# A spectral tokenizer on one core: the row inverse inside the main loop, row transform and mixing in banks of their own, mixing at 32 columns

## The chip, the cores and the metric

The kernel runs on one core of a Trainium2 chip. The metric is device time in microseconds (us) of one execution; lower is better. The kernel before has a median of 5176.1 us over 3 runs (5170.6 to 5191.34).

## What is computed

Sixty-four images of 64 x 64 pixels with 3 channels go through a tokenizer of four Fourier layers and then through two transformer-like blocks (attention, gated experts). Only the tokenizer is touched. Its reference, cut:

```python
h = layer_norm(x @ fc0_w + fc0_b)                # 32 channels
for i in range(4):
    X = rfft2(h)                                 # over the 64 x 64 pixels
    Y[:12, :12]  = einsum('bixy,ioxy->boxy', X[:12, :12],  w1[i])
    Y[-12:, :12] = einsum('bixy,ioxy->boxy', X[-12:, :12], w2[i])
    h = irfft2(Y) + einsum('bchw,oc->bohw', h, conv_w[i]) + conv_b[i]
    h = layer_norm(h)                            # over channels
    if i < 3: h = gelu(h)
h = gelu(h @ fc1_w + fc1_b); h = gelu(h @ fc2_w + fc2_b); h = h @ fc3_w + fc3_b
```

Everything is fp32. The kernel computes the Fourier transforms as products with small tables, and only for the 24 x 12 modes that are kept.

## The kernel before, in words

The images are worked on in 4 groups (loop over `g`) of 16, each group in two units (`u` = 0, 1) of 8 images. A unit's activations stay in `h`. A stage of a unit consists of these steps, which TensorE (PE) carries out in the order in which they are written, each filling PSUM banks that VectorE (DVE) and ScalarE (ACT) empty:

- **row inverse** (`pe_inverse`, L398 to L412, product L408): 8 banks of 16 products with the table `inv_r`, alternately in `aux[0]` and `aux[1]`; `drain_inverse` (L578) copies the even ones to `zq` on DVE and the odd ones on ACT. At its end PE waits until all are copied (L411).
- **main loop** (`pe_main`, L414): 16 chunks of 512 columns in six banks (`main[0..3]`, `aux[0..1]`): column inverse from `zq` (L431, two row halves at a time) plus pointwise convolution of `h` (L434). ACT squares a chunk (L696), DVE sums (L678), POOL or DVE (`dve_newton`) makes the inverse root, DVE scales into `xn` (L669). Five chunks later (`LAG`) PE transposes it back (L442) into `tp[0]`, ACT applies gain and GELU and writes `h` (L708), PE transposes `h` (L450) into `tp[1]`, and ACT copies that to `pix` (L714). The last iterations of the loop, c = 16 to 21, have no chunk products left, only the two transposes ("the tail" below).
- **forward** (`pe_forward`, L454): the column transform A (L481, 8 banks of 8 products in `aux`, copied to `t_w`), the row transform B (L496, 4 banks of 12 products in `aux`, each copied to `xs` by four copies of 32 partitions), and the mixing of channels (L510, 6 banks of 24 products in `aux`, weights `mixw` of 64 columns, two output halves in turn). Each product streams 64 columns of `xs`, of which the upper 32 are overwritten by the next product. Before mixing, PE waits until all of B has been copied (L500). `drain_forward` (L586) copies on DVE (j = 0) and ACT (j = 1); at its end DVE makes a negated copy (L627), on which SyncE's queue (SP) waits (`sp_spectrum`, L759): it writes the mixed spectrum to DRAM in 8 transfers and loads it back transposed into `yd`, from which the next row inverse of the same unit reads.

Stage 0 (embedding) has no inverse: its chunks are L424, and it transposes `h` afterwards (L467) instead of in the loop. Then a hardware loop runs over three layers `l`, each for both units (inverse, main, forward); the fourth layer (`last`) has inverse and main alone, and an MLP (L544, L554, L563) ends the group. So a group has 8 forwards, 8 inverses and 10 main loops. Counters (`aux_full`, `aux_free`, `main_free`, ...) order the engines; `base_of` gives their values. An fp32 product is two records each of weight load and of product in the profile.

Of the kernel before, what the change touches and what calls it, by code (L numbers as in the profile page):

```python
# [15 lines left out]
LAYERS, M1, M2 = 4, 12, 12  # L16
# [12 lines left out]
AX_EMBED, AX_ROWS, AX_A, AX_B, AX_MIX, AX_C = 1, 4, 4, 2, 3, 4  # L29
# [3 lines left out]
AX_LAYER = UNITS * (AX_C + AX_FWD)  # L33
AX_LAST = UNITS * AX_C
AX_GROUP = AX_STAGE0 + (LAYERS - 1) * AX_LAYER + AX_LAST + UNITS * AX_MLP

# [71 lines left out]
def tokenizer(nc, t, tok, named):  # L108
# [9 lines left out]
    with ctx:  # L118
# [17 lines left out]
        XC = KX * KQ * 2 * MODE  # L136
        xs = sb("xs", [128, XC + MODE])

# [14 lines left out]
        start = sb("start", [1, 24])  # L153
# [53 lines left out]
        with nc.Block() as block:  # L207
# [116 lines left out]
            def _(pe):  # L324
# [4 lines left out]
                for l in range(LAYERS):  # L329
# [7 lines left out]
                                  "tp_full", "tp_free"))  # L337
        aux_full = [sem(f"aux_full{i}") for i in range(2)]
# [15 lines left out]
        xv = xs[:, 0:XC].rearrange("p (x n b k a) -> p x n b k a", x=KX, n=2 * KQ, b=NB, k=4)  # L354
# [7 lines left out]
        def base_of(g, s, u, l=None):  # L362
# [8 lines left out]
            return chunks, g * AX_GROUP + (START + done + u * (AX_C if s == LAYERS else AX_LAYER // 2))  # L371
# [26 lines left out]
        def pe_inverse(pe, g, s, u, l):  # L398

            _, n = base_of(g, s, u, l)  # L400
            stage = l if l is not None else s - 1
            pe.wait_ge(yd_in[u], (g * LAYERS + stage + 1) * 16)
            for k in range(2 * AX_C):
                j, a, e = k % 2, k // 2, k % 2
                pe_aux(pe, j, n + k // 2)
                for i in range(8):
                    for half in range(2):
                        mm = pe.matmul(aux[j][64 * half:64 * half + 48, 64 * i:64 * i + 64], ydv[:, u, 8 * e + i, :, :, a].rearrange("p s n -> p (s n)"),  # L408
                                       inv_r[:, 64 * half:64 * half + 64], start=True, stop=True, skip_group_check=True)
                mm.then_inc(aux_full[j], 1)  # L410
            for j in range(2):  # L411
                pe.wait_ge(aux_free[j], n + AX_C)  # L412

        def pe_main(pe, g, s, u, l):  # L414

            m, _ = base_of(g, s, u, l)
            layer = l if l is not None else s - 1
            turns = l is not None
            for c in range(NCH + LAG + (1 if turns else 0)):
                if c < NCH:  # L420
                    bank = wide[c % 6]
                    if s == 0:
# [22 lines left out]
                if turns and c > LAG:  # L445
# [6 lines left out]
                    mm.then_inc(turn_full, 1)  # L452

        def pe_forward(pe, g, s, u, l):  # L454
            m, n = base_of(g, s, u, l)
            if s == 0:
# [17 lines left out]
            else:  # L474
                n = n + AX_C
# [1179 lines left out]
```

## Time and profile before

| | before |
|---|---|
| median of 3 runs | 5176.1 us |
| the profiled execution | 5172.52 us |
| its span | 5170.7 us |
| PE busy | 4003.1 us (77%) |
| PE weight loads busy | 3068.6 us (59%) |
| DVE busy | 2241.4 us (43%) |
| ACT busy | 2084.0 us (40%) |
| POOL busy | 1057.9 us (20%) |
| granted PE clock, mean | 0.904 |

The page of the profile gives shares of the whole span, in which the tokenizer's stages and the blocks behind it are mixed. What a change in one stage is worth is read from that stage: its rows on the time axis, the gaps before them (in brackets, with who ended them), and the clock in those microseconds.

### The profile page before, as it was taken

The page shows a single profiled execution, that of the slowest core. Times are in us where ns is not written, and L with a number is a line of the kernel's source. Part 1 is how long each engine was busy: PE and PEld are TensorE (multiplying, and loading weights), DVE is VectorE, ACT ScalarE, POOL GpSimd, SP SyncE. Part 2 cuts the span into 40 slices and gives each one's busy share as a digit, 9 for nine tenths or more (in the row PEclk, how much of TensorE's full clock was granted, in tenths as well). Part 3 has the DMA queues.
Part 4 walks back from the last instruction along what each step waited for, and adds up shares of the span by engine and source line. Part 5 has one row for each costly group of instructions (what it writes and reads, how often), then busy time and mean ns, then how long its engine had stood idle before and what let it go on. Part 6 is the DMA issues. An engine that isn't in the chain of part 4 may idle for free. (4 is left out here: it accounts for less than half of the span.)

```text
span 5170.7 us, 101350 instructions
## 1 busy us (share of the span) xinstructions
PE 4003.1 (77%) x39344; PEld 3068.6 (59%) x39344; DVE 2241.4 (43%) x4535; ACT 2084.0 (40%) x3050; POOL 1057.9 (20%) x700
## 2 busy tenths in 40 slices
PE   0278888896788888967888889778888896867258
PEld 0167777742677777526777775267777751763146
DVE  6543433431434334315334334153343331687666
ACT  1243443355434433555334335553343355221112
POOL 0122321321213212203122123031231230000120
PEclk9989999998899999888999999889999988878679
DMA  9402102200021012000120120001201201000000
GB/s 214 135 20 75 57 20 66 66 1 15 19 73 59 20 57 75 1 15 20 59 73 20 57 65 11 14 21 56 75 20 57 74 1 30 2 1 0 0 1 9
DMA packets 168686, 213.28 MB, mean 41 GB/s; under 512 B 156402, under 2 KB 158679, under 8 KB 159874
## 3 DMA queue, kind: packets, MB, share of 16 engines
q1 hardware_dynamic: 166514, 182.84, 12.1%
q10 hardware_dynamic: 1680, 23.60, 1.8%
q8 instruction: 343, 5.62, 0.5%
q14 instruction: 149, 1.22, 0.1%
HBM read 147.28 MB, written 59.12 MB: 40 GB/s over the span
## 5 line engine op out<-in xcount | busy, mean ns | idle before, releaser
L725 POOL TENSOR_TENSOR rstd<-var,mhalf 128x16 f32<-128x16 f32 x320 | 931.2, 2910 | 44.1 <-POOL var L722 4.4
L722 POOL TENSOR_TENSOR var<-ssum,eps 128x16 f32<-128x16 f32 x320 | 69.4, 217 | 3179.7 <-DVE ssum L678 3179.7
L678 DVE TENSOR_REDUCE ssum<-sq 128x16 f32<-128x512 f32 x640 | 437.6, 684 | 502.5 <-ACT sq L696 493.1
L708 ACT ACTIVATE h<-tp,gb 128x512 f32<-128x512 f32 x640 | 550.5, 866 | 144.4 <-PE tp L442 141.6
L442 PE MATMUL tp<-ident,xn 128*128 128x128 f32 x2560 | 434.3, 299 | 182.6 <-DVE xn L669 113.0
L442 PEld LDWEIGHTS tp<-ident,xn 128*128 128x128 f32 x2560 | 326.7, 154 | 294.0 <-DVE xn L669 207.4
L481 PE MATMUL aux<-fwd_w,pix 128*128 128x96 f32 x4096 | 469.7, 277 | 23.2 <-ACT pix L714 16.2
L434 PEld LDWEIGHTS main<-convw,h 128*128 128x128 f32 x3072 | 391.9, 202 | 154.8 <-issue 154.8
L481 PEld LDWEIGHTS aux<-fwd_w,pix 128*128 128x128 f32 x4096 | 464.7, 194 | 30.5 <-ACT pix L714 21.9
L696 ACT ACTIVATE sq<-main 128x512 f32<-128x512 f32 x480 | 288.2, 600 | 474.7 <-PE main L434 425.0
L569 DVE COPY t_w<-aux 128x384 f32<-128x384 f32 (+1 forms) x224 | 105.7, 472 | 792.5 <-PE aux L481 491.2
L434 PE MATMUL main<-convw,h 128*128 (+1 forms) x3072 | 440.5, 293 | 0.0
L408 PE MATMUL aux<-inv_r,yd 96*48 96x64 f32 x8192 | 387.7, 262 | 40.6 <-issue 40.6
L408 PEld LDWEIGHTS aux<-inv_r,yd 96*48 96x48 f32 x8192 | 382.6, 189 | 44.7 <-issue 44.7
L510 PE MATMUL aux<-xs,mixw 128*64 128x64 f32 x9216 | 322.9, 240 | 86.1 <-ACT xs L569 86.1
L569 ACT COPY t_w<-aux 128x384 f32<-128x384 f32 (+1 forms) x224 | 91.9, 410 | 735.5 <-PE aux L481 428.1
L510 PEld LDWEIGHTS aux<-xs,mixw 128*64 128x64 f32 x9216 | 319.4, 153 | 90.4 <-issue 90.4
L431 PE MATMUL main<-zq,inv_w 48*128 48x512 f32 x768 | 282.8, 661 | 64.6 <-DVE xn L669 38.2
L669 DVE TENSOR_TENSOR xn<-main,rstd 128x512 f32<-128x512 f32 x480 | 324.2, 682 | 17.5 <-PE tp L442 14.0
L450 PE MATMUL tp<-ident,h 128*128 128x128 f32 x1536 | 235.7, 277 | 23.5 <-ACT pix L714 23.5
L569 DVE COPY xs<-aux 32x288 f32<-32x288 f32 x256 | 164.4, 642 | 169.4 <-PE aux L496 166.8
L714 ACT COPY pix<-tp 128x512 f32<-128x512 f32 x384 | 221.3, 576 | 17.9 <-PE tp L450 17.9
(223 smaller groups left out, 5547.3 us busy)
## 6 DMA issues: line engine op xcount, KB each, us to landing
mixw<-mix_scratch SPq DMA_DIRECT2D x16, 4608.0 KB, 18.7
y_scratch<-t_w SPq DMA_DIRECT2D x256, 144.0 KB
yd<-y_scratch SPq DMA_DIRECT2D x32, 1152.0 KB, 7.3
mix_scratch<-mixw SPq DMA_DIRECT2D x64, 288.0 KB, 4.7
mixw<-mix_scratch ACTq DMA_DIRECT2D x1, 4608.0 KB, 13.7
h<-in_L_tok_w1r ACTq DMA_DIRECT2D x6, 576.0 KB, 10.4
h<-in_L_tok_w1i ACTq DMA_DIRECT2D x6, 576.0 KB, 10.3
h<-in_L_tok_w2r ACTq DMA_DIRECT2D x6, 576.0 KB, 18.3
```

The source lines that it names most:

```text
L408: mm = pe.matmul(aux[j][64 * half:64 * half + 48, 64 * i:64 * i + 64], ydv[:, u, 8 * e + i, :, :, a].rearrange("p s n -> p (s n)"), inv_r[ ...
L431: pe.matmul(wide[(c + half) % 6][:, :], inv_w[rows, :], zq[rows, 256 * c:256 * c + 512], start=True, stop=False)
L434: mm = pe.matmul(bank[:, 128 * i:128 * i + 128], h[:, (u * S + 4 * c + i) * 128:(u * S + 4 * c + i) * 128 + 128], convw[:, layer, :] if l ...
L442: mm = pe.transpose(tp[0 if turns else d % 2][:, 128 * i:128 * i + 128], xn[:, d % 2, 128 * i:128 * i + 128], ident[:, :])
L481: mm = pe.matmul(aux[j][:, 48 * i:48 * i + 96], pv[:, c0 + i, 2 * ap:2 * ap + 2, :].rearrange("p a r -> p (a r)"), fwd_w[:, :], start=True ...
L510: mm = pe.matmul(aux[j][64 * half:64 * half + 64, MODE * x:MODE * x + 2 * MODE], mv[:, half, part, x0 + x, y, :], xs[:, at:at + 2 * MODE], ...
L569: return eng.tensor_copy(out, in_) if j == 0 else eng.copy(out, in_)
L669: dve.tensor_tensor(xn[:, d % 2, :].rearrange("p (n c) -> p n c", c=CH), wide[d % 6][:, :].rearrange("p (n c) -> p n c", c=CH), rstd[:, d ...
L678: dve.tensor_reduce(ssum[:, c % 4, :], sq[:, c % 2, :].rearrange("p (n c) -> p n c", c=CH), AX.X, ALU.add).then_inc(red_done, 1)
L696: act.activation(sq[:, c % 2, :], wide[c % 6][:, :], ACT.Square, scale=CH ** -0.5 / (CUBIC if c % 4 >= 2 else 1)).then_inc(sq_full, 1)
L708: act.activation(out, in_, fn, bias=gb[:, 1, stage:stage + 1] if l is None else gb[:, 1, bass.ds(stage, 1)], scale=gb[:, 0, stage:stage + ...
L725: pool.tensor_tensor(rstd[:, c % 4, :], var[:, c % 4, :], mhalf[:, :], ALU.pow).then_inc(rstd_done, 2)
```

## The change

Three edits. (1) The row inverse is no longer a step of its own ahead of a unit's main loop. It is issued inside the main loop of the unit before it, from iteration 15 on: one bank each in c = 15 to 18, two each in c = 19 and 20 (`inv_banks`), behind the transposes of that iteration, with counters of its own (`inv_full`, `inv_free`). DVE empties its banks between the last three scalings, ACT behind its copy to `pix`. Unit 1's inverse lies in unit 0's loop, unit 0's next one in unit 1's loop. Stage 0's second unit takes the first inverse. (2) A uses `main[0..1]`. B is grouped by thirds of the column modes: six banks of its own (`row_bank`), four products each, each bank copied by four copies of 32 partitions as before (24 copies of 32 x 192 in all instead of 16 of 32 x 288). `xs` is laid out by those thirds, and the mixing of a third waits only for its two banks; mixing too has six banks of its own (`mix_bank`), and the next main loop waits for them bit by bit (`AUX_AT`). (3) A mixing product streams 32 columns instead of 64. The numbers of products are the same throughout.

```diff
-AX_EMBED, AX_ROWS, AX_A, AX_B, AX_MIX, AX_C = 1, 4, 4, 2, 3, 4
+AX_EMBED, AX_ROWS, AX_A, AX_B, AX_MIX, AX_C = 1, 4, 4, 3, 3, 4
...
-        XC = KX * KQ * 2 * MODE
-        xs = sb("xs", [128, XC + MODE])
+        XC = 2 * KX * MODE
+        xs = sb("xs", [128, KQ * (XC + MODE)])
...
+        def inv_of(g, u, stage):
+
+            return g * (LAYERS * UNITS * AX_C) + stage * (UNITS * AX_C) + (START + u * AX_C)
+
+
+        def inv_banks(c):
+            return {NCH - 1: (0,), NCH: (1,), NCH + 1: (2,), NCH + 2: (3,), NCH + 3: (4, 5), NCH + 4: (6, 7)}.get(c, ())
...
+        def mix_bank(k):
+            return (main[0], main[1], main[2], main[3], tp[0], tp[1])[k]
+
+        def row_bank(y, b):
+            return ((main[2], main[3]), tp, aux)[y][b]
...
+        def pe_inverse(pe, g, u, stage, m, k):
+
+            j, a, e = k % 2, k // 2, k % 2
+            n = inv_of(g, u, stage)
+            if k == 0:
+                pe.wait_ge(yd_in[u], g * (LAYERS * 16) + stage * 16 + 16)
+                pe.wait_ge(main_free, m + 12)
+            pe.wait_ge(inv_free[j], n + k // 2)
+            for i in range(8):
+                for half in range(2):
+                    mm = pe.matmul(aux[j][64 * half:64 * half + 48, 64 * i:64 * i + 64], ydv[:, u, 8 * e + i, :, :, a].rearrange("p s n -> p (s n)"),
+                                   inv_r[:, 64 * half:64 * half + 64], start=True, stop=True, skip_group_check=True)
+            mm.then_inc(inv_full[j], 1)
...
+        AUX_AT = {0: 2, 2: 1, 4: 0}
...
+            if s > 0:
+                for j in range(2):
+                    pe.wait_ge(inv_free[j], inv_of(g, u, layer) + AX_C)
             for c in range(NCH + LAG + (1 if turns else 0)):
                 if c < NCH:
                     bank = wide[c % 6]
+                    if s > 0 and c in AUX_AT:
+                        for j in range(2):
+                            pe.wait_ge(aux_free[j], n - AUX_AT[c])
...
+                if nxt is not None:
+                    for k in inv_banks(c):
+                        pe_inverse(pe, g, *nxt, m, k)
+
+        def pe_forward(pe, g, s, u, l, nxt):
             m, n = base_of(g, s, u, l)
+            if nxt is not None:
+                for j in range(2):
+                    pe.wait_ge(inv_free[j], inv_of(g, *nxt) + AX_C)
...
-                    mm = pe.matmul(aux[j][:, 48 * i:48 * i + 96],
+                    mm = pe.matmul(main[j][:, 48 * i:48 * i + 96],
                                    pv[:, c0 + i, 2 * ap:2 * ap + 2, :].rearrange("p a r -> p (a r)"),
                                    fwd_w[:, :], start=True, stop=True, skip_group_check=True)
                 mm.then_inc(aux_full[j], 1)
+            done = n
             n = n + AX_A
-            for j in range(2):
-                pe.wait_ge(aux_free[j], n)
+            for y in range(KQ):
+                for b in range(NB):
+                    rows = row_bank(y, b)[:, 0:192].rearrange("p (s a n) -> p s a n", s=2, a=2)
+                    for ap in range(2):
+                        if y == 0 and b == 0:
+                            for j in range(2):
+                                pe.wait_ge(aux_free[j], done + AX_A // 2 * (ap + 1))
+                        for part, table in enumerate((fwd_re, fwd_im)):
+                            mm = pe.matmul(rows[:, :, ap, :], tv[:, ap, b, part, 4 * y:4 * y + 4].rearrange("p k c -> p (k c)"),
+                                           table[:, :], start=(part == 0), stop=(part == 1), skip_group_check=True)
+                    mm.then_inc(aux_full[b], 1)
 
             if u == 0:
                 pe.wait_ge(mixw_in, (g * LAYERS + (0 if s == 0 else (l + 1)) + 1) * 16)
-            for k in range(2 * AX_B):
-                j, ap, b = k % 2, k // 2, k % 2
-                pe_aux(pe, j, n + k // 2)
-                for y in range(KQ):
-                    for part, table in enumerate((fwd_re, fwd_im)):
-                        mm = pe.matmul(aux[j][:, 96 * y:96 * y + 96], tv[:, ap, b, part, 4 * y:4 * y + 4].rearrange("p k c -> p (k c)"),
-                                       table[:, :], start=(part == 0), stop=(part == 1), skip_group_check=True)
-                mm.then_inc(aux_full[j], 1)
-            n = n + AX_B
-            for j in range(2):
-                pe.wait_ge(aux_free[j], n)
             for k in range(2 * AX_MIX):
                 j, y, x0 = k % 2, k // 2, M1 // 2 * (k % 2)
-                pe_aux(pe, j, n + k // 2)
+                bank = mix_bank(k)
+                if j == 0:
+                    for b in range(NB):
+                        pe.wait_ge(aux_free[b], n + y + 1)
                 for x in range(M1 // 2):
                     for part in range(2):
                         for half in range(2):
-                            at = (((half * M1 + x0 + x) * KQ + y) * 2 + part) * MODE
+                            at = y * (XC + MODE) + (part * KX + half * M1 + x0 + x) * MODE
                             flat = k == 0 and x == 0 and half == 0
-                            mm = pe.matmul(aux[j][64 * half:64 * half + 64, MODE * x:MODE * x + 2 * MODE],
-                                           mv[:, half, part, x0 + x, y, :], xs[:, at:at + 2 * MODE],
+                            mm = pe.matmul(bank[64 * half:64 * half + 64, MODE * x:MODE * x + MODE],
+                                           mv[:, half, part, x0 + x, y, :], xs[:, at:at + MODE],
                                            start=(part == 0), stop=(part == 1 and not flat), skip_group_check=True)
                     if k == 0 and x == 0:
-                        mm = pe.matmul(aux[j][0:64, 0:MODE], biasw[:, :],
+                        mm = pe.matmul(bank[0:64, 0:MODE], biasw[:, :],
                                        dc[:, 0, :] if s == 0 else dc[:, bass.ds(l + 1, 1), :].rearrange("p l n -> p (l n)"), start=False, stop=True, skip_group_check=True)
                 mm.then_inc(aux_full[j], 1)
...
+        def drain_inverse(eng, j, g, u, stage, k):
+            n = inv_of(g, u, stage)
+            a, e = k // 2, k % 2
+            eng.wait_ge(inv_full[j], n + (k // 2 + 1))
+            copy(eng, j, zv[0:112, :, a, :, e, :],
+                 aux[j][0:112, :].rearrange("p (i d r) -> p r d i", i=8, d=2)).then_inc(inv_free[j], 1)
...
-            for k in range(j, 2 * AX_B, 2):
-                ap, b = k // 2, k % 2
-                eng.wait_ge(aux_full[j], n + (k // 2 + 1))
+            for y in range(KQ):
+                eng.wait_ge(aux_full[j], n + y + 1)
                 for ky in range(4):
                     rows = slice(32 * ky, 32 * ky + 32)
-                    out = xv[rows, :, :, b, ky, 2 * ap:2 * ap + 2].rearrange("p x n a -> p n a x")
-                    ins = copy(eng, j, out, aux[j][rows, 0:288].rearrange("p (n a x) -> p n a x", n=2 * KQ, a=2))
+                    ins = copy(eng, j, xv[rows, y, :, :, j, ky, :].rearrange("p s x a -> p s a x"),
+                               row_bank(y, j)[rows, 0:192].rearrange("p (s a x) -> p s a x", s=2, a=NA))
                 ins.then_inc(aux_free[j], 1)
             n = n + AX_B
             for k in range(j, 2 * AX_MIX, 2):
                 y, x0 = k // 2, M1 // 2 * (k % 2)
                 eng.wait_ge(aux_full[j], n + (k // 2 + 1))
                 copy(eng, j, yv[:, x0:x0 + M1 // 2, :, 4 * y:4 * y + 4, :].rearrange("p x b k a -> p (x b) (k a)"),
-                     aux[j][:, 0:192].rearrange("p (m z) -> p m z", z=4 * NA)).then_inc(aux_free[j], 1)
+                     mix_bank(k)[:, 0:192].rearrange("p (m z) -> p m z", z=4 * NA)).then_inc(aux_free[j], 1)
...
+                if nxt is not None:
+                    drain_inverse(dve, 0, g, *nxt, 2 * (d - NCH + 3))
+            if nxt is not None:
+                drain_inverse(dve, 0, g, *nxt, 6)
...
+                if nxt is not None:
+                    for k in inv_banks(c - 1):
+                        if k % 2:
+                            drain_inverse(act, 1, g, *nxt, k)
+            if nxt is not None and not turns:
+                drain_inverse(act, 1, g, *nxt, 7)
...
+                        nxt = (0, 0) if u == 1 else None
                         pe_embed(pe, g, u)
-                        pe_main(pe, g, 0, u, None)
-                        pe_forward(pe, g, 0, u, None)
+                        pe_main(pe, g, 0, u, None, nxt)
+                        pe_forward(pe, g, 0, u, None, nxt)
 
                 def layer(g, l):
                     for u in range(UNITS):
-                        pe_inverse(pe, g, 1, u, l)
-                        pe_main(pe, g, 1, u, l)
-                        pe_forward(pe, g, 1, u, l)
+                        nxt = (1, l) if u == 0 else (0, l + 1)
+                        pe_main(pe, g, 1, u, l, nxt)
+                        pe_forward(pe, g, 1, u, l, nxt)
 
                 def last(g):
                     for u in range(UNITS):
-                        pe_inverse(pe, g, LAYERS, u, None)
-                        pe_main(pe, g, LAYERS, u, None)
+                        pe_main(pe, g, LAYERS, u, None, (1, LAYERS - 1) if u == 0 else None)
```

## Rows read from the trace of the kernel before

**Rows 1.** Windows of a unit's six steps: length; PE, PEld, DVE, ACT, POOL busy; PEclk, DMA, GB/s.

```profile
404.02:416.63 12.61, 11.68 (x262) 11.55 (x258) 3.53 (x5) 3.94 (x6) 0.00 (x0) 1.00 0.53 124
416.63:453.71 37.08, 35.28 (x244) 26.91 (x245) 22.81 (x56) 23.01 (x38) 24.36 (x16) 1.00 0.41 151
453.71:464.02 10.31, 6.01 (x44) 4.68 (x44) 3.99 (x13) 7.18 (x12) 0.53 (x1) 1.00 0.01 2
464.02:479.48 15.46, 14.53 (x128) 14.40 (x129) 2.23 (x4) 1.92 (x4) 0.00 (x0) 1.00 0.01 2
479.48:489.34 9.86, 5.81 (x48) 5.51 (x49) 5.13 (x8) 5.08 (x8) 0.00 (x0) 1.00 0.00 0
489.34:499.40 10.06, 10.06 (x291) 10.06 (x293) 1.07 (x3) 0.64 (x2) 0.00 (x0) 0.83 0.01 3
```

**Rows 2.** Timeline of the same unit's tail: start, length, what; gap and its ender in brackets.

```profile
453.71 0.63 PE L442 MATMUL tp<-ident,xn 128*128 128x128 f32 x4 [0.60 <-ACT h L708]
...
459.73 0.78 ACT L708 ACTIVATE h<-tp,gb 128x512 f32<-128x512 f32 x1 [0.41 <-PE tp L442]
...
464.02 14.53 PE L481 MATMUL aux<-fwd_w,pix 128*128 128x96 f32 x128 [0.68 <-ACT pix L714]
```

**Rows 3.** Groups of one unit's time: copies; count, busy us, mean ns, idle before.

```profile
L569 ACT COPY zq<-aux 112x512 f32<-112x512 f32 x4 | 2.3, 586 | 8.1 <-PE aux L408 8.1
...
L569 DVE COPY xs<-aux 32x288 f32<-32x288 f32 x8 | 5.1, 642 | 5.5 <-PE aux L496 5.4
```

**Rows 4.** The issue and landing of a spectrum: timeline row, and the page's part 6.

```profile
414.31 0.32 SPq L769 DMA_DIRECT2D yd<-y_scratch  x1
...
yd<-y_scratch SPq DMA_DIRECT2D x32, 1152.0 KB, 7.3
```

**Rows 5.** Timeline of the MLP: two changes between array shapes.

```profile
1125.79 1.14 PE L544 MATMUL main<-h,f1w 32*128 32x512 f32 x8
1126.86 1.94 PE L554 MATMUL tp<-t_w,f2w 128*64 128x512 f32 x8
...
1128.73 1.54 PE L544 MATMUL main<-h,f1w 32*128 32x512 f32 x8
```

**Rows 6.** Timeline of the other tails: stage 0's second unit, the last layer's first unit.

```profile
348.97 1.91 PE L442 MATMUL tp<-ident,xn 128*128 128x128 f32 x8
...
359.25 1.97 PE L467 MATMUL aux<-ident,h 128*128 128x128 f32 x8 [1.35 <-ACT h L708]
...
1044.30 0.66 PE L442 MATMUL tp<-ident,xn 128*128 128x128 f32 x4 [0.24 <-DVE xn L669]
...
1064.07 1.13 PE L431 MATMUL main<-zq,inv_w 48*128 48x512 f32 x4 [0.73 <-issue]
```

**Rows 7.** All waits and all groups of PE: before mixing, before B, mixing itself.

```profile
PE aux L510 <- ACT xs L569: 86.1, 32, 2.7
...
L496 PE MATMUL aux<-fwd_re,t_w 128*128 128x96 f32 x768 | 152.4, 280 | 68.0 <-DVE xs L569 43.6 <-ACT t_w L569 14.6 <-issue 9.8
...
L510 PE MATMUL aux<-xs,mixw 128*64 128x64 f32 x9216 | 322.9, 240 | 86.1 <-ACT xs L569 86.1
```

**Rows 8.** Windows, the mixing products (L510) alone: start of a mixing, rest.

```profile
489.50:492.50 3.00, 3.00 (x57) 3.00 (x58) 0.50 0.02 5
493.00:499.00 6.00, 6.00 (x214) 6.00 (x212) 1.00 0.01 3
```

**Rows 9.** L330 in timeline and groups: 128 weight columns, 32 streamed.

```profile
172.27 1.89 PE L330 MATMUL aux<-xs 32*128 32x32 f32 x8
...
L330 PE MATMUL aux<-xs 32*128 32x32 f32 x8 | 1.9, 396 | 0.0
```

**Rows 10.** Windows, products of 64 rows x 64 columns (L1474) in a later block.

```profile
4946.00:4953.00 7.00, 7.00 (x126) 7.00 (x126) 1.00 0.01 2
```

**Rows 11.** Timeline of a main loop that begins at the lower clock, and the A behind it.

```profile
809.85 1.83 PE L431 MATMUL main<-zq,inv_w 48*128 48x512 f32 x4 [0.91 <-ACT zq L569]
...
862.00 8.17 PE L481 MATMUL aux<-fwd_w,pix 128*128 128x96 f32 x71 [0.68 <-ACT pix L714]
```

More of the change, by code:

```diff
@@ L32 @@
 AX_STAGE0 = UNITS * (AX_EMBED + AX_ROWS + AX_FWD)
[L33 to L35 removed]
+AX_LAYER = UNITS * AX_FWD
+AX_GROUP = AX_STAGE0 + (LAYERS - 1) * AX_LAYER + UNITS * AX_MLP
 NEWTON_OPS = 9
@@ L152, in tokenizer @@
         newton_w = sb("newton_w", [128, 4, 16])
-        start = sb("start", [1, 24])
+        start = sb("start", [1, 28])
         fwd_w = sb("fwd_w", [128, 96])
@@ L337, in tokenizer @@
                                   "tp_full", "tp_free"))
+        inv_full = [sem(f"inv_full{i}") for i in range(2)]
+        inv_free = [sem(f"inv_free{i}") for i in range(2)]
         aux_full = [sem(f"aux_full{i}") for i in range(2)]
@@ L396, in pe_embed, with pe_main @@
                 pe.wait_ge(aux_free[j], n + 1)
[L398 to L404, printed above, removed]
-                pe_aux(pe, j, n + k // 2)
[L406 to L409, printed above, removed]
-                mm.then_inc(aux_full[j], 1)
-            for j in range(2):
-                pe.wait_ge(aux_free[j], n + AX_C)
-        def pe_main(pe, g, s, u, l):
-            m, _ = base_of(g, s, u, l)
+        def pe_inverse(pe, g, u, stage, m, k):
[11 more added lines that the diff above has]
+        AUX_AT = {0: 2, 2: 1, 4: 0}
+        def pe_main(pe, g, s, u, l, nxt):
+            m, n = base_of(g, s, u, l)
             layer = l if l is not None else s - 1
             turns = l is not None
+            if s > 0:
+                for j in range(2):
+                    pe.wait_ge(inv_free[j], inv_of(g, u, layer) + AX_C)
             for c in range(NCH + LAG + (1 if turns else 0)):
@@ L576, in drain_embed @@
             copy(eng, j, xt_of(u)[0:96, 512 * j:512 * j + 512], aux[j][0:96, :]).then_inc(aux_free[j], 1)
-        def drain_inverse(eng, j, g, s, u, l):
-            _, n = base_of(g, s, u, l)
-            for k in range(j, 2 * AX_C, 2):
-                a, e = k // 2, k % 2
-                eng.wait_ge(aux_full[j], n + (k // 2 + 1))
-                copy(eng, j, zv[0:112, :, a, :, e, :],
-                     aux[j][0:112, :].rearrange("p (i d r) -> p r d i", i=8, d=2)).then_inc(aux_free[j], 1)
+        def drain_inverse(eng, j, g, u, stage, k):
[4 more added lines that the diff above has]
+                 aux[j][0:112, :].rearrange("p (i d r) -> p r d i", i=8, d=2)).then_inc(inv_free[j], 1)
         def drain_forward(eng, j, g, s, u, l):
@@ L607, in drain_forward @@
                 out = tv[:, ap, :, :, :, c0:c0 + 8].rearrange("p b s k c -> p (b s k) c")
-                copy(eng, j, out, aux[j][:, 0:384].rearrange("p (c n) -> p n c", c=8)).then_inc(aux_free[j], 1)
+                copy(eng, j, out, main[j][:, 0:384].rearrange("p (c n) -> p n c", c=8)).then_inc(aux_free[j], 1)
             n = n + AX_A
-            for k in range(j, 2 * AX_B, 2):
-                ap, b = k // 2, k % 2
-                eng.wait_ge(aux_full[j], n + (k // 2 + 1))
+            for y in range(KQ):
+                eng.wait_ge(aux_full[j], n + y + 1)
                 for ky in range(4):
                     rows = slice(32 * ky, 32 * ky + 32)
-                    out = xv[rows, :, :, b, ky, 2 * ap:2 * ap + 2].rearrange("p x n a -> p n a x")
-                    ins = copy(eng, j, out, aux[j][rows, 0:288].rearrange("p (n a x) -> p n a x", n=2 * KQ, a=2))
+                    ins = copy(eng, j, xv[rows, y, :, :, j, ky, :].rearrange("p s x a -> p s a x"),
+                               row_bank(y, j)[rows, 0:192].rearrange("p (s a x) -> p s a x", s=2, a=NA))
                 ins.then_inc(aux_free[j], 1)
```

25 lines of the change are left out of this document (8 added, 17 removed).

## The prediction

> **What bounds the kernel now.** I read first the page's shares (PE 77% busy, the others under 45%), then the time axis of one unit in windows [rows 1]: six steps that add to 95.38 us. PE is what moves the end in five of them, either working or waiting for a copy that follows its own work; 32 such rounds, one per forward, make up most of the span. In [rows 1] the reader is to see where PE does not work although the step is its own: 0.93 us behind the inverse, 4.30 us in the tail, 4.05 us in B. The tail is paced by a round trip PE, ACT, PE: each transpose waits for ACT's `h` of the chunk before, 0.78 us long, after a gap of 0.6 us [rows 2]. B stops twice for its copies. The last row of [rows 1] shows a third loss: PE is busy for all 10.06 us of mixing, yet its granted clock is 0.83. The windows over the mixing products alone say why [rows 8]: it begins at 0.50 of the clock (1.2 GHz of 2.4) with 57 records in 3 us, and goes on at 1.00 with 214 in 6 us. Before it fell, PE had stood still twice within the 9.86 us of B, 2.7 us of it right ahead of mixing [rows 7].
>
> **Edit 1, the inverse laid into the tail.** Removed: the inverse step of 12.61 us and the tail of 10.31 us [rows 1], with 0.60 us of waiting ahead of the tail's first row [rows 2]: 23.5 us. In their place PE has, from the end of iteration 15: 8 inverse banks, 11.68 us as in [rows 1]; 11 groups of transposes (5 of L442, 6 of L450) at 0.44 us, which is 8 of their records at the 0.109 us that a 128-column record takes in A and here (14.53 us / 128 = 0.1135 for A's [rows 2], so at most that), 4.8 us; changes of array shape; and waits. For the changes: in the MLP a round of 8 products on 32-row quarters and 8 on 64-column halves takes 2.94 us from start to start [rows 5]; the streams alone are 2 and 4 record times of 512 columns, 512 x 2 / 2.4 GHz = 0.427 us each, 2.56 us. Two changes cost 0.38 us. The inverse enters and leaves six times (banks 4, 5 and 6, 7 go in pairs): 2.3 us. For the waits: within the pairs PE needs the ACT copy of the bank two before, which stands in ACT's queue behind `h` and the copy to `pix`; 0.2 us twice. At the end one wait is new: forward waits for bank 7's copy, which ACT makes only after the last copy to `pix`. The old gap there was 0.68 us [rows 2], the copy is 0.586 us [rows 3] and its start costs a little more: 1.4 us. Sum 11.7 + 4.8 + 2.3 + 0.4 + 1.4 = 20.6 us, a gain of 2.9 us. ACT has 0.78 + 0.58 + 0.59 = 1.95 us per iteration against PE's 2.7, so it follows; DVE's added copies (4 of 0.69) stand between scalings that PE asks for 2.7 us apart instead of 1.7. 24 rounds of this kind (three layers, two units, four groups): **70 us**.
>
> The Trainium skill speaks against this edit: TensorEngine Tiling (Array Packing), Key Properties, says that changing the tiling mode, not merely the tile, drains TensorE. The rows agree and give the size: without the changes the gain would be 5.2 us a round, and 55 us more over the 24.
>
> The other 8 inverses lie in tails without L450. In the last layer's first unit the stretch from the first tail transpose to the next main loop is 19.77 us, with the gap ahead of it 20.0 [rows 6]. New: 11.7 + 5 x 0.44 + 2.3 + 0.2 + a wait of 1.0 for bank 7 = 17.4. Gain 2.6 x 4 = **10 us**. In stage 0's second unit the tail from behind the first four records of the row at 348.97 to 359.25 is 9.4 us [rows 6], and the inverse behind it 12.6: 22.0 against 17.4 + 0.8 for records at the lower clock at its start. Its L467 products also begin at the lower clock (1.97 us for 8 [rows 6]); with a full PE ahead they won't, about 1.8 us. Gain 5.5 x 4 = **22 us**.
>
> The data are there in time: the spectrum that the moved inverse reads was written one forward earlier; its load is issued 10 us after mixing and lands 7.3 us later [rows 4], while iteration 15 ends some 39 us after that issue [rows 1]. SP's order is not changed. `zq` is rewritten only after the last chunk has been read. The first bank also waits for chunk 11's scaling, which DVE ended before iteration 15 was over. No cost for these; the cover is 32 us wide.
>
> **Edit 2, B by thirds.** The 2.69 us ahead of mixing (86.1 us in 32 times [rows 7]) and the 1.36 us within B (43.6 us [rows 7]) go, if the copies keep ahead. They do: PE needs 5.4 us for B's 48 records in one run. A bank is copied by four copies; a copy of 32 x 288 was 642 ns [rows 3], one of 32 x 192 lies between 430 ns (by elements) and 642 (if it were all fixed cost). At the dear end DVE's third bank is copied 8.7 us after B's start, ACT's 9.6, and the third third of mixing, which needs them, starts at 10.8 us; the first third starts at 5.4 and needs copies that end at 4.4. So both ends of that bound cost nothing. Of the wait ahead of B (14.6 + 9.8 us [rows 7]) half goes, since the first two products need only A's first half: 12 us. The changes of shape into mixing and out of it, so far covered by waits, now cost 0.19 us each: 12 us. Together 86 + 44 + 12 - 12 = **130 us**. What is late next is the weight load itself: A, B and mixing are one dense run. Six banks for mixing remove nothing, for there was no wait there; the waits that they add at chunks 0, 2 and 4 of the next loop ask for copies long made.
>
> **The clock.** Mixing takes 322.9 / 32 = 10.09 us [rows 7]. At the pace of its second part, (6 + 0.24) / 214 = 29.2 ns a record [rows 8], 288 records take 8.4 us. With no pause ahead of it the clock should not have fallen: 1.7 x 32 = **54 us**.
>
> **Edit 3, 32 columns.** Bounds: if the streamed columns set the pace, 29.2 ns become 14.6 and 32 mixings gain 134 us; if the weight load (64 columns, unchanged) does, nothing. I take nothing. A's records load 128 columns and stream 96 in 113 ns [rows 2], the transposes load 128 and stream 128 in 109: fewer streamed columns are not faster. L330 loads 128 and streams 32, and its eight records are 213 ns apart ((1.89 - 0.396) / 7 [rows 9]), with durations of the lower clock's kind: still the load's pace. Mixing loads half as many columns, into two halves in turn.
>
> The Trainium skill's TensorE: Matmul & The Clock Gate, section "Wait — 56ns, not 53.3ns?", has a start-to-start floor of about 25 ns however few columns are streamed. By it no more than 4 ns a record, 38 us in all, could be gained here; no row shows a pace below 29 ns.
>
> **Sum.** 70 + 10 + 22 + 130 + 54 = 286 us. The profiled execution took 5172.5 us, 3.6 below the median of the three runs. Predicted: **4886 us**.
>
> **Rivals.** (a) *The clock falls in mixing*, because it streams half the columns. Then its records keep the 57 / 3 us pace of [rows 8], (3 + 0.3) / 57 = 57 ns, 16.4 us instead of 8.4, and the next main loop begins at the lower clock. Such a loop took 52.15 us [rows 11] against 37.08 + 10.31 = 47.39 [rows 1]; part of the 4.76 is also met today, so I take 3.2. 11.2 x 32 = 358 us: **5244 us**, slower than before. It decides from 26 of the 32 mixings on (286 / 11.2). Against it: the L1474 products stream 64 columns every 57 ns or so, no more columns per us than mixing will, and the clock stayed at 1.00 for 7 us of them [rows 10]. For it: nothing in the trace streams 32 columns at full clock. If it falls in a part only, 5000 to 5100 us.
> (b) *The overlay brings nothing*: the tail's 4.3 us of idle time are spent on changes and on waits for ACT, because a 64-column shape between 128-column transposes costs more than in the MLP (1.0 us a round trip instead of 0.38), 4886 + 102 = **4990 us**.
> (c) *Mixing does get faster*, by half or all of edit 3's upper bound: **4752 to 4819 us**.
> (d) *B still waits*, since the new layout of `xs` makes a copy dearer than 642 ns (from 0.74 us on the third third is late). At 1.0 us a copy the wait ahead of it is 4 us, which in turn lets the clock fall: 4886 + 128 + 54 = **5068 us**. It would be the change not doing what it says.
>
> **How the numbers follow.** Chances: forecast 0.66 (its own terms give 4830 to 4940), (a) in full 0.04 and in part 0.07, (b) 0.10, (c) 0.09, (d) 0.04. The range 4800 to 5020 holds the forecast, (b) and the near half of (c), 0.8 with some of the forecast's error. A measurement of this kernel can tell about 0.5% from no change. Faster by over 0.5% (below 5150): all but (a) in full and a little of its part, 0.94; within 0.5%: 0.02; slower: 0.04.
>
> **What the changed profile would show.** Edit 1: no L408 between mixing and L431; the stretch from the first tail transpose to A about 20 us, with gaps before L442 gone and about 1.4 us ahead of A. Edit 2: L496 in one run of 5.4 us, no gap ahead of L510. Clock: PEclk 1.00 in the mixing windows, 34 records per us from the first us. Edit 3: that same pace; 60 or more per us would be (c), 17 with PEclk 0.50 (a). Copies to `xs` at 430 to 640 ns; above 740 is (d). A round of PE near 86 us instead of 95. I would be wrong if the loop-end rounds, whose code stalls are not among my rows, lengthened, or if ACT fell behind in the tail.

## The result and the profile after

The changed kernel takes 4903.8 us (median of 4 runs, 4889.6 to 4915.4), the kernel before 5173.4 us beside it. The ratio is 0.9474, with a 95% interval of 0.9437 to 0.9511. The prediction was 4886 us with a range of 4800 to 5020: sign, size and range held. The sum behind it did not hold in every term. Two costs that it did not have, a lower clock in A and longer chunks, took 49 and 54 us; the removed step and the new banks gave back more than they were priced at.

The round of [rows 1] in the profile after, as windows over its steps: chunks, tail with the inverse in it, A, B, mixing. The columns are those of [rows 1].

```profile
398.65:439.31 40.66, 38.56 (x244) 29.57 (x244) 22.96 (x56) 24.00 (x39) 23.69 (x16) 0.92 0.52 175
439.31:459.13 19.82, 18.37 (x301) 16.88 (x301) 7.37 (x18) 9.80 (x17) 1.20 (x1) 1.00 0.01 3
459.13:475.10 15.97, 15.97 (x128) 15.97 (x129) 2.23 (x4) 1.44 (x3) 0.00 (x0) 0.89 0.00 1
475.10:480.98 5.88, 5.67 (x51) 5.44 (x49) 4.22 (x9) 3.86 (x8) 0.00 (x0) 1.00 0.00 0
480.98:489.61 8.63, 8.63 (x292) 8.59 (x291) 2.71 (x7) 3.07 (x7) 0.00 (x0) 1.00 0.01 4
```

Read it against [rows 1] line by line. The inverse's own line of 12.61 us is gone. The tail grew from 10.31 to 19.82 us, and PE works in nearly all of it. B fell from 9.86 to 5.88 us and mixing from 10.06 to 8.63, with the clock at 1.00 instead of 0.83. But two lines went the wrong way. A takes 15.97 us at a mean clock of 0.89, where it took 15.46 at 1.00, waiting included. And the chunks take 40.66 us at 0.92 (in the kernel before this unit needed 36.5 up to the same point, 416.63 to 453.11, at full clock).

The tail itself, one iteration and the end, on the timeline:

```profile
439.31 1.66 PE L423 MATMUL aux<-inv_r,yd 96*48 96x64 f32 x32
440.90 0.66 PE L464 MATMUL tp<-ident,xn 128*128 128x128 f32 x4
441.39 0.60 PE L472 MATMUL tp<-ident,h 128*128 128x128 f32 x4
441.92 1.66 PE L423 MATMUL aux<-inv_r,yd 96*48 96x64 f32 x32
...
457.02 0.66 PE L472 MATMUL tp<-ident,h 128*128 128x128 f32 x4
459.13 16.13 PE L508 MATMUL main<-fwd_w,pix 128*128 128x96 f32 x128 [1.45 <-ACT zq L598]
```

An inverse bank and the two transposes around it follow each other without a gap, 2.61 us from bank to bank. The round trip PE, ACT, PE of [rows 2] is covered. What is left is one wait, 1.45 us, in front of A, for the copy of the last inverse bank.

All stretches of the span by step, from the starts of the steps on PE's timeline, four groups together (us). At the end of a pass of the layer loop PE stalls, for 3.1 to 4.6 us in the kernel before and 4.2 to 4.9 in the changed one, where the profile shows nothing that it waits for; this "code stall" is counted in the step ahead of it. In this table the chunks end with the last product of iteration 15, and the tails begin there, so that iteration 15's two transposes, 0.87 us, count with the tail; in the windows above they count with the chunks:

| step | before | after | difference |
|---|---|---|---|
| row inverse as a step (32) | 423.0 | 0 | -423.0 |
| tails of the layer loops (24) | 285.6 | 495.1 | +209.5 |
| main loops of stage 0 (8), their L467 behind | 397.9 | 418.4 | +20.5 |
| main loops of the last layer (8) | 356.0 | 383.3 | +27.3 |
| **overlay, together** | | | **-165.7** |
| chunks of the layer loops (24) | 881.2 | 935.5 | +54.3 |
| A (32) | 494.1 | 508.7 | +14.6 |
| B (32) | 315.5 | 188.1 | -127.4 |
| mixing (32) | 348.6 | 314.6 | -34.0 |
| sum | | | -258.2 |

The spans differ by 5170.7 - 4913.6 = 257.1 us, so nothing else has moved.

### The profile page after: what moved, and what is told of

Same layout as the page of the kernel before. It is cut to its first block and busy times, and to the rows that moved or that the text cites. A ratio compares the mean times of both kernels' runs of the same rounds, so it can differ in the third digit from the quotient of the medians.

```text
span 4913.6 us, 101922 instructions
## 1 busy us (share of the span) xinstructions
PE 4008.5 (82%) x39344; PEld 3080.9 (63%) x39344; DVE 2260.9 (46%) x4667; ACT 2096.9 (43%) x3178; POOL 1057.9 (22%) x700
## 5 line engine op out<-in xcount | busy, mean ns | idle before, releaser
L508 PE MATMUL main<-fwd_w,pix 128*128 128x96 f32 x4096 | 513.9, 293 | 42.1 <-ACT zq L598 35.1
L508 PEld LDWEIGHTS main<-fwd_w,pix 128*128 128x128 f32 x4096 | 509.6, 209 | 48.8 <-ACT pix L743 40.1
L456 PEld LDWEIGHTS main<-convw,h 128*128 128x128 f32 x3072 | 407.4, 209 | 161.2 <-issue 161.2
L456 PE MATMUL main<-convw,h 128*128 (+1 forms) x3072 | 455.7, 300 | 0.0
L423 PE MATMUL aux<-inv_r,yd 96*48 96x64 f32 x8192 | 417.1, 256 | 9.5 <-DVE zq L598 4.5
L598 DVE COPY t_w<-main 128x384 f32<-128x384 f32 (+1 forms) x192 | 94.2, 490 | 558.3 <-PE main L508 477.4
L598 ACT COPY t_w<-main 128x384 f32<-128x384 f32 (+1 forms) x192 | 81.6, 425 | 580.1 <-PE main L508 479.7
L598 DVE COPY zq<-aux 112x512 f32<-112x512 f32 x128 | 88.1, 688 | 265.6 <-PE aux L423 265.6
L573 PE MATMUL main<-h,f1w 32*128 32x512 f32 x1024 | 181.5, 671 | 14.1 <-ACT pix L768 9.6
L539 PE MATMUL main<-xs,mixw 128*64 128x32 f32 x6144 | 188.9, 223 | 0.0
## 6 DMA issues: line engine op xcount, KB each, us to landing
h<-in_L_tok_w1r ACTq DMA_DIRECT2D x6, 576.0 KB, 10.1
```

The source lines that it names most:

```text
L456: mm = pe.matmul(bank[:, 128 * i:128 * i + 128], h[:, (u * S + 4 * c + i) * 128:(u * S + 4 * c + i) * 128 + 128], convw[:, layer, :] if l ...
L508: mm = pe.matmul(main[j][:, 48 * i:48 * i + 96], pv[:, c0 + i, 2 * ap:2 * ap + 2, :].rearrange("p a r -> p (a r)"), fwd_w[:, :], start=Tru ...
L598: return eng.tensor_copy(out, in_) if j == 0 else eng.copy(out, in_)
```

## The experiments

Each kernel changes one thing, in the changed kernel or in the kernel before, unless it says otherwise. Ratios are to the kernel before, timed beside each on the same chip; the changed kernel's own is 0.9474.

**The wait ahead of A.** The copies of the last inverse bank matter only to `aux`, which the row transform uses in its last third. The edit moves the wait there.

```diff
-            if nxt is not None:
+            if nxt is not None and s == 0:
                 for j in range(2):
                     pe.wait_ge(inv_free[j], inv_of(g, *nxt) + AX_C)
...
             for y in range(KQ):
+                if y == 2 and s > 0 and nxt is not None:
+                    for j in range(2):
+                        pe.wait_ge(inv_free[j], inv_of(g, *nxt) + AX_C)
```

> The changed kernel with one wait moved: in the three layer stages PE waits for the copies of the last inverse banks only before the row-transform banks that lie in the same PSUM banks (aux), not before the column transform A. Theory P (the pause ahead of A lets the clock fall): the wait ahead of A shrinks from 1.45 us to about 0.7 us as in the kernel before, A shrinks from 16.0 to about 14.5 us because its clock stays at 1.00, 24 times 2.2 us, some 50 to 60 us less than the changed kernel's 4904: about 4848. Rival Q (the clock falls because the tail now consists partly of inverse products that fill only part of the array, whatever the pause): the wait shrinks, A stays at 16 us, only 24 x 0.75 = 18 us: about 4886.

Measured: 4858.7 us, ratio 0.9405 (0.939 to 0.942), 45 us less than the changed kernel. The row of A, and two windows after its start, with the clock in the third column from the right:

```profile
454.97 7.27 PE L508 MATMUL main<-fwd_w,pix 128*128 128x96 f32 x63 [0.68 <-ACT pix L746]
...
454.97:458.97 4.00, 4.00 (x36) 4.00 (x36) 0.56 (x1) 0.58 (x2) 0.00 (x0) 1.00 0.00 0
458.97:462.00 3.03, 3.03 (x30) 3.03 (x29) 0.56 (x1) 0.33 (x1) 0.00 (x0) 1.00 0.00 0
```

against these of the changed kernel, whose A begins at 459.13:

```profile
459.00:460.00 1.00, 0.87 (x8) 0.90 (x8) 0.00 (x0) 0.00 (x0) 0.00 (x0) 0.97 0.00 0
460.00:463.00 3.00, 3.00 (x17) 3.00 (x15) 0.56 (x1) 0.00 (x0) 0.00 (x0) 0.50 0.00 0
463.00:464.00 1.00, 1.00 (x9) 1.00 (x9) 0.00 (x0) 0.00 (x0) 0.00 (x0) 0.82 0.00 0
```

The wait is back to 0.68 us and all 24 A of the layer loops take 14.4 us instead of 16.0 to 17.6. The inverse products are in the tail as they were, so their shape alone does not lower the clock; without the longer pause it does not fall. The pause costs 0.77 us by itself and 2.05 us on average through the clock (16.42 - 14.37), in 24 places: 68 us. The medians differ by 45 only, and the spans of the two profiled executions by 61, among other things because the chunks of the last layer's eight loops took 11 us more in this one: they lost the clock in six of the eight, in the changed kernel in one.

The length of the pause does not decide alone, though. Of the 24 A behind a wait of 1.45 us, none kept the clock in the changed kernel, but 4 did in each of two experiments below (the table load, the pause ahead of mixing) and 11 in the overlay alone. And in the kernel before, 3 of its 24 lost it behind 0.68 us, at the end of a tail that stood still for 4.3 us in pieces.

**The table load.** ACT loads a function table twice per pass of the layer loop, at the head of the pass and ahead of the first GELU. In the kernel before the first of the two fell into the inverse step. Now it stands between chunk 0 and its square (timeline of the changed kernel):

```profile
400.97 1.28 ACT L725 ACT_TABLE_LOAD   x1 [2.09 <-PE main L456]
402.26 1.09 ACT L725 ACTIVATE sq<-main 128x512 f32<-128x512 f32 x2
...
408.80 1.28 ACT L737 ACT_TABLE_LOAD   x1 [0.32 <-PE tp L464]
...
411.65 0.75 PE L453 MATMUL main<-zq,inv_w 48*128 48x512 f32 x1 [2.00 <-DVE xn L694]
```

The edit issues a tiny GELU at the head of the first unit's loop, whose result nobody reads. It draws the load forward. It does one thing more: the table loaded for a GELU serves the squares too, so the second load goes, and the execution has 20 loads instead of 32.

```diff
+            if turns and u == 0:
+                act.activation(warm[:, :], mhalf[0:1, 0:4], ACT.Gelu)
```

> The changed kernel with one tiny GELU on ACT at the start of each layer's first unit, whose result nobody reads: it makes ACT load its table there, not between the first chunk and its square. Theory P (the table load of 1.28 us, which lay in the inverse step before and was covered there, now delays the first squares, so DVE's scaling of chunk 1 and with it PE's chunk 6): the first square starts some 2.3 us after the loop's first product instead of 3.6, PE's wait ahead of chunk 6 shrinks in 12 loops from 2.00 us to the 1.2 to 1.4 us of the other loops, the clock is low for a shorter time; 12 x (0.7 + 0 to 2) = 8 to 32 us, about 4885. Rival Q (the 2.00 us are set by DVE's own order of reduces and root steps): nothing changes but the place of the load, 4904.

Measured: 4885.3 us, ratio 0.9461 (0.9445 to 0.9478). The interval overlaps the changed kernel's, so alone the gain cannot be told from nothing. Together with the late wait it can:

> Both edits together, the late wait ahead of the row banks and the early table load. If both theories hold the gains add: about 4830 (50 to 60 plus 8 to 32 us below 4904), and the ratio to the kernel before is 0.93 to 0.936. If only the pause matters 4848, if only the table 4885, if neither 4886 to 4904.

Measured: 4844.2 us, ratio 0.937 (0.9357 to 0.9383), against 0.9405 (0.939 to 0.942) for the late wait alone: 14 us by the medians, 18 by the ratios, and 8 between the two profiled executions, all of it in the chunks of the layer loops. In the timeline of this kernel the load lies beside PE's first products (which begin at 397.43), the first square comes 2.3 us after them instead of 3.6, and the wait ahead of chunk 6 is 1.19 us as in the kernel before:

```profile
397.78 1.28 ACT L726 ACT_TABLE_LOAD   x1
399.76 0.60 ACT L731 ACTIVATE sq<-main 128x512 f32<-128x512 f32 x1 [0.49 <-PE main L457]
...
409.30 1.12 PE L454 MATMUL main<-zq,inv_w 48*128 48x512 f32 x2 [1.19 <-DVE xn L698]
```

The gain seems to belong to the first load. The second was in the kernel before as well (426.47), and the chunks of a loop at full clock take 35.6 us there with it and in this kernel without it. Nor were there twelve waits of 2.00 us to shorten: in the changed kernel 7 of the 12 first-unit loops have one, and in the other 5, all of them behind a code stall, PE waits 1.19 to 1.29.

The Trainium skill (ScalarE: Activation LUTs, What ACT_TABLE_LOAD costs) gives about 1283 ns for the load, as the row shows, and about as much again for a drain, 2.66 us in all. The trace shows no second part here: in the changed kernel the square starts as the load ends.

**Overlay alone, and rows alone.** The first keeps edit 1 and puts B, mixing and `xs` back as they were. The second is the kernel before with edits 2 and 3 and no other.

> Edit 1 alone: the row inverse inside the main loop, column transform in main[0..1], but row transform and mixing in aux with their waits and with 64 streamed columns, as in the kernel before. The forecast's own terms give 102 us less than before: about 5065. Theory P (of these, the lower clock in A behind the new wait takes 24 x 1.5 us and the table load another 10 to 30): 5080 to 5120, A at 16 us. Rival Q (the edits only pay together, since the overlay needs the short row transform): no change against the kernel before, 5150 to 5190.

> Edits 2 and 3 alone: six banks for the row transform and six for mixing, 32 streamed columns, the inverse as a step of its own as in the kernel before. Theory P: B 5.9 us instead of 9.9, mixing 8.6 instead of 10.1, so 32 x 5.4 = 175 us less than before, minus nothing else: about 4995. With the result of the overlay alone it adds up to the changed kernel's 260. Rival Q (the main loop's chunks got longer in the changed kernel because a dense run of products now lies ahead of them): here the inverse lies ahead as before and the chunks keep their 36.7 us on average; if they rise to 39 here too, the cause lies in B and mixing.

Measured: overlay alone 5076.7 us, ratio 0.9837 (0.982 to 0.9853), with the same tails as the changed kernel (20.64 us). Rows alone 4980.4 us, ratio 0.9647 (0.9631 to 0.9663), B 5.88 us. The gains add: 0.0163 + 0.0353 = 0.0516 against 0.0526 for the whole. So the edits do not need each other. The overlay alone gave 86 us, where its terms in the forecast make 102, and the rows alone 183. In the rows-alone kernel the layer chunks take 37.0 us on average and A 14.37; in the overlay-alone kernel 37.8 and 16.6, of which 0.77 us is the wait ahead of B. Rival Q of the second expectation is thus half answered: B and mixing by themselves leave the chunks as long as they were (36.7); with the overlay they grow, and most with both (39.0).

**32 columns, in both kernels.** The first experiment puts the changed kernel's mixing back to 64 columns, the second the kernel before to 32.

```diff
-                            mm = pe.matmul(bank[64 * half:64 * half + 64, MODE * x:MODE * x + MODE],
-                                           mv[:, half, part, x0 + x, y, :], xs[:, at:at + MODE],
+                            mm = pe.matmul(bank[64 * half:64 * half + 64, MODE * x:MODE * x + 2 * MODE],
+                                           mv[:, half, part, x0 + x, y, :], xs[:, at:at + 2 * MODE],
```

> The changed kernel with its mixing products back at 64 streamed columns, upper half overwritten as in the kernel before; nothing else. Theory P (weight loads of 64 columns set the pace): mixing stays at 8.6 us and 29 ns a record, clock 1.00 in both, time within 0.3% of the changed kernel. Rival Q (32 columns are quicker): mixing longer than 8.6 us, each ns a record is 9 us in all. Rival R (32 columns starve the clock in what follows): with 64 the clock falls less often in the next main loop, and the kernel is 10 to 50 us faster than 4904.

Measured: 4914.8 us, ratio 0.9506 (0.9492 to 0.952). That is 0.3% above the changed kernel's 0.9474, inside its interval. The windows over the mixing products alone, first the changed kernel's (32 columns), then this one's (64):

```profile
482.00:488.00 6.00, 6.00 (x214) 6.00 (x210) 1.00 0.02 5
```

```profile
482.00:488.00 6.00, 6.00 (x214) 6.00 (x212) 1.00 0.01 3
```

Both run 214 records in 6 us, the same as the kernel before in [rows 8]. Half the streamed columns change nothing in the pace. That fits a pace set by the weight load, but no run changes the weight columns, so this part is argued and not shown. Rival R fails too: with 64 columns the kernel is no faster.

> The kernel before with its mixing products at 32 streamed columns, nothing else. Its mixing begins at the lower clock, behind a pause of 2.7 us. Theory P (the weight load sets the pace at either clock and the clock comes back under it): mixing stays at about 10.1 us and the time within 0.5% of before. Rival Q (half the columns don't bring the clock back): all of mixing runs at 57 ns a record, 16.4 us, and the inverse behind it begins low: +6.3 us or more in 32 places, 5370 or more. In between lies a later return of the clock.

Measured: 5187.3 us, ratio 1.0043 (1.0026 to 1.0059): slower by 0.4%. Behind the pause of 2.7 us mixing begins at the lower clock with 32 columns too. It comes back after some 3.5 us in most places and after some 7 in three, whose mixings take 11.2 to 11.5 us instead of 10.1. With 64 columns that happened in two places of the kernel before, with 11.2 and 11.3 us. All mixings together differ by 4.2 us (352.8 against 348.6) of the 15.6 us between the two profiled executions. So at full clock the width is free, while behind a pause the kernel with 32 columns is slower by 0.4%, and only a small part of that is seen in mixing; where the rest comes from stays open.

**The pause ahead of mixing again.** In the changed kernel the first mixing bank waits for all copies of B.

```diff
-                        pe.wait_ge(aux_free[b], n + y + 1)
+                        pe.wait_ge(aux_free[b], n + KQ)
```

> The changed kernel with the first mixing bank waiting for all copies of the row transform instead of those of its own third. The last copy ends 2.6 us after PE could begin. Theory P (it is the pause ahead of mixing that lets the clock fall, and not what B consists of): a gap of about 2.6 us and a mixing that begins at 0.50, 8.6 plus about 1.6 us or more; 32 x 4.2 = 135 us above 4904, about 5040. Rival Q (the clock stays, since the gap is single now): 32 x 2.6 = 83 us, about 4987.

Measured: 5023.9 us, ratio 0.9734 (0.9718 to 0.975), 120 us above the changed kernel. The gap and two windows behind it:

```profile
395.96 0.65 PE L539 MATMUL main<-xs,mixw 128*64 128x32 f32 x8 [2.51 <-ACT xs L598]
...
396.00:402.00 6.00, 6.00 (x114) 6.00 (x115) 0.36 (x1) 0.32 (x1) 0.00 (x0) 0.50 0.01 3
402.00:405.00 3.00, 3.00 (x106) 3.00 (x104) 0.36 (x1) 0.29 (x1) 0.00 (x0) 0.97 0.02 5
```

PE works without a stop for 6 us at 0.50, 114 records where 214 would fit. The gap is 2.5 us, the rest of the 3.75 us per forward is the clock. Here too the pause did not always tell: 3 of the 32 mixings kept the clock behind it. Both of the kernel before's losses around mixing are one pause.

**Filling chunk 6's wait.** The best kernel so far still loses in the chunks: in 23 of its 24 layer loops they take 37 us or more, where a loop at full clock takes 35.6. In front of chunk 6 PE waits 1.2 to 1.4 us for DVE's second scaling. The edit puts products of the identity with itself there, into a bank that is free and overwritten later.

```diff
+                        if c == 6:
+                            for i in range(5):
+                                pe.matmul(tp[1][:, 0:128], ident[:, :], ident[:, :], start=True, stop=True, skip_group_check=True)
                         if c % 2 == 0:
                             for half in range(2):
```

> The kernel with the late wait and the early table load (4844 us), and in every main loop behind an inverse, ahead of chunk 6's first product, five more products of the identity table with itself into the bank tp[1], which is free there and overwritten later: 10 records, 1.1 us of work in a wait of 1.2 to 1.4 us. Theory P (the pause at chunk 6 lets the clock fall, which costs 3 us a loop, as the pauses ahead of A and of mixing did): PE's 16 chunks take 35.6 us in all loops instead of 38.6 on average; 24 x 3 plus some 15 us in the last layer: about 4760. Rival Q (what the clock misses there are full-height products, since L454 uses 48 of 128 rows; or DVE's order sets the length): the chunks keep 38 to 39 us, 4844 to 4860.

Measured: 4772.3 us, ratio 0.9234 (0.9221 to 0.9247). The first line is a window in the kernel without the filling, from 11.3 us after the loop's first product; the second is the same stretch of the same loop with it:

```profile
493.00:501.00 8.00, 7.15 (x27) 5.73 (x28) 3.27 (x6) 1.95 (x3) 6.22 (x4) 0.57 0.45 109
```

```profile
490.78:498.78 8.00, 7.70 (x51) 5.47 (x50) 5.36 (x13) 3.65 (x7) 6.22 (x4) 1.00 0.33 78
```

The clock stays at 1.00. The chunks take 35.5 or 35.6 us in the 16 layer loops that are entered without a code stall and 37.2 in the other 8 (38.0 in one of them). No loop behind an inverse loses the clock at chunk 6 any more. Useless products saved 72 us, since they kept the clock for the useful ones. They use all 128 rows, though; whether products of 48 rows would have done the same, as rival Q asks, no run tells.

> The same with eight products instead of five, 1.75 us of work, some 0.4 us more than the wait. Theory P: the clock never falls at chunk 6 either, but 0.4 us a loop are given back: 32 x 0.4 = 13 us above the run with five, if five were enough; if five were too few, this one is the faster.

Measured: 4769.7 us, ratio 0.9226 (0.9212 to 0.9241), the same as with five. The longer filling was expected to cost 13 us and cost nothing that can be measured. There was more room than the wait of 1.2 us shows: without filling, the four column-inverse products of chunks 6 and 7 stretch over 3.36 us, elsewhere over 1.06, since half of them wait for DVE while the other half are done. With five products as with eight, chunk 6's pointwise products start 12.92 us after the loop's first product, as in the kernel before.

## Why the prediction was right, and where its sum was off

The spans differ by 257 us where 286 were forecast, and such a near hit is partly luck. By the table, the overlay gave 64 us more than its terms and the row transform some 32 more; the clock in A took 49 that no term had, the chunks 54, and mixing gave 20 less.

**Edit 1** was forecast at 102 us and gave 165.7. The mechanism was as described, the new tail too: forecast 20.6 us from the end of iteration 15 to A, measured 19.8 (439.31 to 459.13). In the layer loops the difference has two halves of some 20 us. The tail was 0.8 us shorter than forecast, 24 times. And I priced the inverse step at one unit's 12.61 us; the mean over 32 is 423.0 / 32 = 13.2 and over the 24 of the layer loops 13.4, since behind a code stall it ran at the lower clock and mostly stopped once more. A change of array shape was read from the MLP at 0.38 us for two; here a bank with two transposes takes 2.61 us, 11.68 / 8 + 8 x 0.109 = 2.33 without changes, so 0.28 us a visit. (A group of transposes is four such records, not eight as my sum says; its 0.44 us is right.) The Trainium skill's rule (TensorEngine Tiling (Array Packing), Key Properties) holds: there is a price, and it is small against the 4.3 us of idle time that the visits filled. The last layer was under-sized as well, at 10 us where the table gives some 23, and stage 0 at 22 where it gives some 30. All this is gross: what the overlay did to A and to the chunks stands in other rows, and alone it gained 86 us.

**The new wait ahead of A** was forecast at 1.4 us and is 1.45. What the step lacked was the consequence: it stands in front of the longest dense run of the round, and the clock falls behind it. I had used that very reading of [rows 8] for mixing and did not apply it to the wait that I was adding. By the table the clock cost 24 x 2.05 = 49 us; of this and of the wait, 68 us together, the late wait recovered 45 by the medians.

**The table load** was not among my steps at all, although the step that I removed covered one in 12 of its 32 instances. It cost 8 to 18 us.

**Edit 2** held: the two waits within B were forecast at 130 us, and B is 127 us shorter, at 5.88 us a time. Its text says 5.4 us for B's run, which PE's 5.81 us of work in [rows 1] already contradicted. The wait ahead of B, 24 us, of which I gave away half, went whole. It is counted in A: with the rows alone all A together took 459.6 us against 494.1. So edit 2 was worth some 160 us, and the lower clock behind the new wait hid a part of it. A 32 x 192 copy takes 0.50 us (four in 1.99), between my ends of 0.43 and 0.64, and no third of mixing waits.

```profile
387.47 1.99 DVE L598 COPY xs<-tp 32x192 f32<-32x192 f32 x4
```

**The clock in mixing** held: 10.06 to 8.63 us with PEclk 1.00. The gain by the table is 34 us against 54, because PE's code stall, counted there, grew from 3.8 to 4.6 us on average in 8 places, mixing takes 0.2 us more than the bare pace, and four of the kernel before's mixings had run at full clock already.

**Edit 3** held at nothing. Rival (a) did not happen: no mixing of the changed kernel ran at the lower clock. In the kernel before, where a pause lies ahead of mixing, 32 columns did cost 0.4%; in the changed kernel, where edit 2 has removed that pause, they cost nothing that can be measured. Rival (c) fell with the equal counts of records; the Trainium skill's floor of 25 ns (TensorE: Matmul & The Clock Gate, "Wait — 56ns, not 53.3ns?") was not reached at 32 columns, the pace staying at 29. Rivals (b) and (d) fell with the tail and the copies.

**The chunks**, 54 us longer, were no term of mine. Part is the table load. The rest is the clock, as the filling shows. Of the 24 layer loops, 13 had the full clock in the 4 us behind chunk 6's wait in the kernel before, 2 in the changed kernel, 11 in the overlay alone and 12 with the rows alone. The eight loops of the last layer went the other way: 4 had it before, 7 in the changed kernel. The wait there is nearly the same in all four kernels (1.19 to 1.56 us where no table load precedes it), so what makes the same pause cost more often stays open. I have no experiment that separates the dense run ahead of the loop from the later start of DVE and ACT in it. Whatever tips it, filling the pause ends it.

## What to carry to other kernels

When a step is removed, list what else it covered: here a table load. When a wait is added, look at what runs behind it: a wait of 1.45 us in front of a dense run cost more through the clock than through its own length, while the same copies waited for in the next step cost nothing. When a forecast comes out right, add up its terms against the profile all the same: here five misses nearly cancelled. If PE must wait a microsecond or two between dense runs, products that nobody needs can be cheaper than standing still; try it where the granted clock drops behind the gap.

## What the runs showed of the hardware that I had not expected

- A pause of 1.45 us was enough for the granted clock to fall from 1.00 to 0.50 for some 3 to 7 us of the dense work behind it: A at 0.50 took 17 records in 3 us where 30 fit at 1.00. It did so ahead of all 24 A of the changed kernel, but of 20, 20 and 13 of 24 in three of the experiments. Behind 0.68 us at the same place none fell with the late wait, and 3 of 24 in the kernel before.
- The same pause of 1.2 to 1.4 us ahead of chunk 6 lowered the clock in some loops and not in others of one and the same execution.
- Behind a pause of 2.7 us, mixing ran at half clock for some 3.5 us in most places and for some 7 in a few: in three of 32 with 32 streamed columns, in two of 32 with 64.
- A GELU issued ahead of the squares left one table load per pass of the loop instead of two.
- The width of the stream (32, 64) had no effect on the pace of products with 64 weight columns: 214 records in 6 us at either.
